# Rounding half of each query pair's phases on VectorE instead of ScalarE, in a fused attention, context and quantised-layer kernel

## The reference, cut to what matters

```python
def _fourier_kernel(x, proj_mat):
    p = jnp.einsum('blhd,dm->blhm', x, proj_mat) / math.sqrt(D_HEAD)
    return jnp.concatenate([jnp.cos(p), jnp.sin(p)], axis=-1) / math.sqrt(D_KMAP)
q = (x @ Wq.T + bq).reshape(Bv, Lv, N_HEAD, D_HEAD)
k = (x @ Wk.T + bk).reshape(Bv, Lv, N_HEAD, D_HEAD)
v = (x @ Wv.T + bv).reshape(Bv, Lv, N_HEAD, D_HEAD)
kv = jnp.einsum('blhm,blhd->bhmd', _fourier_kernel(k, proj_mat), v)
out = jnp.einsum('blhm,bhmd->blhd', _fourier_kernel(q, proj_mat), kv)
return out.reshape(Bv, Lv, D_MODEL) @ Wo.T + bo
```

## Time and profile before

| | |
|---|---|
| three runs | 1849.26 us median (1847.9 to 1851.37) |
| profiled execution | 1849.84 us, of which the span is 1848.1 us |
| mean granted clock of TensorE | 0.956 of full speed |
| PE / DVE / ACT / POOL busy | 1657.3 / 1311.1 / 1149.4 / 711.3 us |

### The profile page before, as it was taken

The page is one execution under the profiler, slowest core; times in us unless marked ns, Lnnn a source line. Parts: engine busy times, 40 slices in busy tenths (PEclk is TensorE's granted clock), DMA queues, the critical chain, the costliest instruction groups (busy, mean ns, idle before and its releaser), DMA issues. The chain is left out here.

```text
span 1848.1 us, 31958 instructions
## 1 busy us (share of the span) xinstructions
PE 1657.3 (90%) x12210; PEld 1175.4 (64%) x12210; DVE 1311.1 (71%) x1821; ACT 1149.4 (62%) x1510; POOL 711.3 (38%) x641
## 2 busy tenths in 40 slices
PE   4998998998999899899899989965698898899995
PEld 3755765675676577567467657733466776677784
DVE  4575766757667666765766767687588878888885
ACT  2595776777577577667857757755145554555564
POOL 3031212404313130340431313053286767777776
PEclk9999999999999999999999999987799999999998
DMA  4100202202011020220201102013211212222201
GB/s 152 47 24 1 70 2 69 69 1 70 25 46 44 27 70 1 69 69 1 70 24 47 42 29 70 1 46 111 80 49 56 79 63 75 74 68 74 69 35 57
DMA packets 49102, 95.87 MB, mean 52 GB/s; under 512 B 3472, under 2 KB 3792, under 8 KB 48976
## 3 DMA queue, kind: packets, MB, share of 16 engines
q1 hardware_dynamic: 38864, 76.29, 13.1%
q10 hardware_dynamic: 10112, 17.69, 2.6%
HBM read 60.38 MB, written 33.59 MB: 51 GB/s over the span
## 5 line engine op out<-in xcount | busy, mean ns | idle before, releaser
L698 DVE SCALAR_TENSOR_TENSOR feat<-feat,phases 128x1024 f32<-128x1024 f32 x256 | 301.0, 1217 | 197.2 <-ACT feat L595 197.2
L595 ACT ACTIVATE feat<-phases 128x1024 f32<-128x1024 f32 x256 | 248.3, 1023 | 217.6 <-PE phases L457 123.7
L602 ACT ACTIVATE feat<-feat 128x1024 f32<-128x1024 f32 x256 | 271.5, 1061 | 84.9 <-DVE feat L698 76.0
L385 POOL TENSOR_TENSOR ln<-moments,eps 128x4 f32<-128x4 f32 x16 | 3.2, 202 | 741.4 <-DVE moments L747 741.4
L608 ACT ACTIVATE feat<-feat 128x1024 f32<-128x1024 f32 x256 | 256.9, 1047 | 17.0 <-DVE feat L705 16.9
L705 DVE TENSOR_SCALAR feat<-feat 128x1024 int32<-128x1024 int32 x256 | 213.9, 840 | 47.9 <-ACT feat L602 47.7
L446 PE MATMUL bank<-wo_hi,att_hi 128*128 128x512 f32 x256 | 110.9, 433 | 51.3 <-DVE att_lo L731 43.0
L544 PE MATMUL kv_sum<-feat,kv_cols 128*32 128x512 f32 x1024 | 126.4, 612 | 8.6 <-ACT feat L608 8.6
L372 POOL TENSOR_TENSOR res<-res,bo_all 128x512 f32<-128x512 f32 x64 | 85.2, 1359 | 118.9 <-DMA res<-x 118.4
L446 PE MATMUL bank<-xt_hi,win_hi 128*128 128x512 f32 x256 | 109.2, 427 | 19.4 <-POOL xt_lo L363 19.4
L518 PE MATMUL kv_sum<-feat,v 128*32 128x256 f32 x2048 | 123.8, 382 | 0.0
(11 more groups left out here) (178 smaller groups left out, 4156.6 us busy)
## 6 DMA issues: line engine op xcount, KB each, us to landing
normed<-res SPq DMA_DIRECT2D x32, 513.0 KB, 4.7
xt_raw<-xT SPq DMA_DIRECT2D x16, 1024.0 KB, 6.2
res<-x SPq DMA_DIRECT2D x32, 512.0 KB, 4.2
xs<-normed SPq DMA_DIRECT2D x24, 513.0 KB, 4.1
out<-xs ACTq DMA_DIRECT2D x24, 512.0 KB, 2.8
feat<-normed SPq DMA_DIRECT2D x8, 513.0 KB, 3.8
out<-feat ACTq DMA_DIRECT2D x8, 512.0 KB, 2.8
fold<-ctx SPq DMA_DIRECT2D x8, 256.0 KB, 3.8
```

Of the source, the lines that this page charges most:

```text
L595: act.activation(feat[2 * (w % 2) + p][:, 0, :], phases[:, 2 * p:2 * p + 2, :].rearrange("p h n -> p (h n)"), ACT.Identity, bias=ROUND).th ...
L602: act.activation(f[:, 1, :], f[:, 0, :], ACT.Sin, scale=-TWO_PI).then_inc(sin_done, 1)
L698: dve.scalar_tensor_tensor(f[:, 0, :], f[:, 0, :], ROUND, phases[:, 2 * p:2 * p + 2, :].rearrange("p h n -> p (h n)"), ALU.subtract, ALU.s ...
```

## The change

In query pairs (`w >= KPAIRS`), ACT rounds only unit 0. DVE rounds unit 1 itself, with one `tensor_scalar` that reads `phases` in PSUM and writes `feat` in SBUF, at the head of its phase step, ahead of the fraction of unit 0. A new semaphore `rounded_here` orders DVE's own two instructions. Key pairs stay as they are, except for the arithmetic of the count that is waited for.

```diff
@@ ACT, kind "phase"
-                        for p in range(2):
+                        for p in range(2 if w < KPAIRS else 1):
                             act.activation(feat[2 * (w % 2) + p][:, 0, :], phases[:, 2 * p:2 * p + 2, :].rearrange("p h n -> p (h n)"),
                                            ACT.Identity, bias=ROUND).then_inc(rounded, 1)
@@ DVE, kind "phase"
                         w = s[1]
+                        if w >= KPAIRS:
+                            f = feat[2 * (w % 2) + 1]
+                            dve.wait_ge(phase_ready, PAIRS_A * own + w + 1)
+                            if w < KPAIRS + 2:
+                                dve.wait_ge(feat_used, KPAIRS * own + w - 1)
+                            dve.tensor_scalar(f[:, 0, :], phases[:, 2:4, :].rearrange("p h n -> p (h n)"), ROUND, None,
+                                              ALU.add).then_inc(rounded_here, 1)
                         for p in range(2):
                             f = feat[2 * (w % 2) + p]
-                            dve.wait_ge(rounded, 2 * (PAIRS_A * own + w) + p + 1)
+                            if p == 1 and w >= KPAIRS:
+                                dve.wait_ge(rounded_here, KPAIRS * own + w - KPAIRS + 1)
+                            else:
+                                dve.wait_ge(rounded, 3 * KPAIRS * own + (2 * w + p if w < KPAIRS else w + KPAIRS) + 1)
```

More of the change, by code:

```diff
@@ L221, in attention @@
         product_done, bank_free, hi_ready = sem("product_done"), sem("bank_free"), sem("hi_ready")
-        phase_ready, rounded, frac_ready = sem("phase_ready"), sem("rounded"), sem("frac_ready")
+        phase_ready, rounded, rounded_here, frac_ready = sem("phase_ready"), sem("rounded"), sem("rounded_here"), sem("frac_ready")
         sin_done, fold_ready = sem("sin_done"), sem("fold_ready")
```

## The result

The changed kernel takes 1882.05 us (median of 4 runs, 1880.01 to 1882.99), the kernel before 1850.32 us on the same chip. The ratio is 1.0168, with a 95% interval of 1.0148 to 1.0188: 32 us slower. The profiled executions differ by 32.9 us of span, 1881.0 against 1848.1.

The account below looks back on a forecast made before the run. PE bounds the stretch from `wo` (0,0); in pairs 8 to 12 it waits for DVE. Six loop batches 28.4 + first batch 4.2 + tail 5.2 = 37.8 us on 1849.26 gave 1887 us, 8-in-10 range 1868 to 1904.

Parts of the forecast that it names:

- The bound and the chain: Pairs 8 to 12: PE waits for the ACT-DVE chain; ACT's second rounding lies beside the first fraction, so removal gains nothing.
- The length of the addition: DVE in query pairs: 1.13 us from the added instruction's start to the fraction's; lower end 0.6, upper end 1.22.
- The cost at each pair: Query pairs: each fraction starts later by 1.13 us minus DVE's idle time ahead of it; 4.73 us a loop batch.
- the idle time: DVE's bracketed wait ahead of the fraction: 0.51 us at pair 9, none at 10, 0.22 at 11 and 12.
- The sign of the sine's wait: Sign of being right: in query pairs the sine L602 waits 0.5 to 1.1 us longer for the fraction L698.
- The first batch: First batch: 0.07 + 0.30 + 3 x 0.91 + 1.09 = 4.2 us, pair 10 taken like pairs 11 and 12.
- The tail: Last batch: pairs 8 to 11 cost 0.07 + 0.62 + 1.13 + 1.13, pairs 13 to 15 0.58, 0.51, 1.13; 5.2 us.
- pair 12, whose delay was called hidden: Tail, pair 12: delay costs nothing, since its two magnitudes take 7.20 us beside a 4.83 us POOL instruction.
- Which delays reach the end: Loop batch: pairs 8 to 12 all count, 3.64 us; 13 and 14 get through by PSUM banks, 1.09; 15 nothing.
- The clock: Rival: longer PE waits cause one more clock fall a batch, 1.8 to 2.5 us; some 1902 us, chance 0.15.
- The sum: Whole kernel: loop batches 28.4, first batch 4.2 and tail 5.2 make 37.8 us slower, forecast 1887 us.

Follow-up runs that it names:

- pairs 8 and 15: VectorE rounds unit 1 in pairs 8 and 15 alone, ScalarE in the others; ratio 1.0008 to the kernel before.
- the kernel with those two alone: VectorE rounds unit 1 in pairs 13 and 14 alone, ScalarE in the others; ratio 1.0034 to the kernel before.
- work on DVE that was worth moving: Kernel before with DVE's last normalisation of a batch moved behind pair 10: 1844.89 us; with phase ahead of output on ACT and DVE too: 1840.82 us.
- the stand-in: Kernel before plus a DVE instruction nobody reads, 1024 values from two constant SBUF rows, ahead of the query pairs' fractions; 1897.33 us, ratio 1.0265.

## Why the prediction was right

**The bound and the chain.** Right. The second rounding was free, shown twice: taken off alone it gave nothing (0.9993), and work put in its place in the changed kernel cost nothing.

**The length of the addition.** Right: 64 instructions of 1205 to 1225 ns, the fraction 1.13 us behind. The Trainium skill ("VectorE: DVE Perf Modes", "Why PSUM operands drop a tier") lets 32-bit work with a PSUM operand run in the slowest tier only. The trace agrees: the magnitude, a `tensor_scalar` of the same size within SBUF, takes 0.69 us alone.

**The cost at each pair,** 1.13 less the idle time. The rule is right, and the sizes of the exposed pairs 9 to 14 were 0.07 to 0.1 us too large:

```
             pair 8   9     10    11    12    13    14    15 (loop)
predicted    0.07    0.62  1.13  0.91  0.91  0.58  0.51  0
measured     0.09    0.53  1.06  0.81  0.81  0.49  0.43  0
```

The term mis-sized is the idle time. The bracket counts it from the recorded end of the instruction ahead, but the next one can start 0.08 us ahead of that end when it waits for nothing (619.55 against 619.63). The addition so gained 0.07 to 0.1 us at every exposed pair. For a loop batch that makes 4.2 us instead of 4.73 (pair 8's 0.09 to pair 14's 0.43), 3 us over six.

**The sign of the sine's wait.** "Larger by 0.5 to 1.1 us in query pairs" was too small. It is 99 us over 64 pairs, 1.5 each, because the gap that the rounding leaves is waiting too. The sum did not use it.

**The first batch** was mis-sized: 4.2 us predicted, 2.7 measured (0.14 + 0.21 + 0.61 + 0 + 0.82 + 0.49 + 0.43). I costed pairs 10 and 11 by the pattern of the earlier trace rows, which says nothing of POOL. In this batch POOL works beside DVE's magnitudes, and it met them at another moment in each of the two profiled executions. Those of pair 9 lasted 2.94 us before and 2.73 after. Those of pair 10, before and then after:

```profile
130.04 3.40 DVE L705 TENSOR_SCALAR feat<-feat 128x1024 int32<-128x1024 int32 x2
```

```profile
130.98 0.89 DVE L715 TENSOR_SCALAR feat<-feat 128x1024 int32<-128x1024 int32 x1
132.11 1.47 DVE L715 TENSOR_SCALAR feat<-feat 128x1024 int32<-128x1024 int32 x1 [0.24 <-ACT feat L602]
```

They ended 5.75 us behind the start of the fraction before and 4.93 after. This 0.8 us is what took pair 11's delay. It is not a property of the addition: with nothing added at all (the rounding taken off alone) pairs 10 and 11 of the first batch add -0.46 and -0.84.

**The tail:** 5.2 us predicted. Measured are 3.7 for pairs 8 to `wo` (0,0) (predicted 2.95), 0.92 for pairs 13 and 14 (predicted 1.09), and 1.14 for pair 15 at its fraction (predicted 1.13). The sum is near for a partly wrong reason. Pair 11 added 2.66 instead of 1.13, for POOL's additions met the second magnitude of pair 10 and a weight's instruction (L666) behind it. Both before, then both after:

```profile
1213.39 1.23 DVE L705 TENSOR_SCALAR feat<-feat 128x1024 int32<-128x1024 int32 x2
...
1215.19 2.28 DVE L666 TENSOR_TENSOR xt_raw<-xt_raw,winv 128x2048 f32<-128x2048 f32 x1
```

```profile
1241.89 2.32 DVE L715 TENSOR_SCALAR feat<-feat 128x1024 int32<-128x1024 int32 x2
...
1244.79 2.70 DVE L666 TENSOR_TENSOR xt_raw<-xt_raw,winv 128x2048 f32<-128x2048 f32 x1
```

That is 1.5 us, and the prediction had nothing for it but its range. Half of it is given back: pair 12, whose delay was called hidden, and `wo` (0,0) together add -0.7 us. Not all of it is due to the addition: three kernels that have none in pairs 10 to 12 (the rounding taken off alone, pairs 8 and 15, pairs 13 and 14) add 0.6 to 1.1 us at pair 11 of the tail and give 0.8 back at pair 12.

**Which delays reach the end.** Right for all seven pairs, pairs 13 and 14 included, which the kernel with those two alone confirms by itself.

**The clock.** The rival falls: what the steps add leaves no room for one more fall of 1.8 to 2.5 us a batch. Between `wo` (0,0) and phases 13 the eight batches add -0.63, 0.85, -1.42, 0.78, -0.20, 1.05, -1.31 and 0.28 us, in sum -0.6, although PE waits longer ahead (5.2 to 5.5 us in all loop batches, 3.6 to 4.3 before; 8.8 in the tail, 12.2 before). Windows of two loop batches and the tail after, to set beside the earlier trace rows:

```profile
627.80:636.00 8.20, 8.15 (x28) 6.22 (x28) 1.39 (x2) 0.00 (x0) 0.00 (x0) 0.68 0.01 2
787.00:794.20 7.20, 7.17 (x28) 5.50 (x28) 1.39 (x2) 0.00 (x0) 0.00 (x0) 0.79 0.01 2
...
1268.90:1277.30 8.40, 8.40 (x24) 6.38 (x24) 1.39 (x2) 0.00 (x0) 1.94 (x1) 0.65 0.01 2
```

The fall of the clock moves to and fro by 1.4 us, and its mean stays.

**The sum:** 28.4 + 4.2 + 5.2 = 37.8 predicted. The parts measured in the profiled execution are 25.3 (six loop batches of 4.2), 2.7 and 5.7, together 33.7. Less the 0.6 of the clock's column that is 33.1, and the execution is 32.9 us late at `wo` (1,0) of the tail. So the 6 us by which the predicted sum was high are the idle time's 3, the first batch's 1.5, less 0.5 by which the tail was low, the clock's 0.6 and 1.4 between this execution and the medians, which differ by 31.7. That the two spans differ by 32.9 too is partly luck. In the kernel with work put back on ScalarE, pair 15's fraction in the tail is 33.9 us late, and its span is only 28.9 us longer (1877.0), so the rest of the program moves by some us of its own from one execution to the next.

## What to carry to other kernels

Moving work from one engine to another pays only if the first engine is waited for at that place. Look at what ends the wait of the instruction behind it: here the sine waited for DVE and not for the rounding, so the rounding was free where it stood. What an added instruction costs is read pair by pair, as its length from start to start less the idle time ahead of its place, and the same rule, used the other way round, found work on DVE that was worth moving, though it promised twice what came. Where a third engine lengthens instructions, here POOL those of DVE, a shift of half a us moves them in or out of its way, and the rule then misses: by 0.8 us at one pair and by 1.5 at another in the changed kernel. An engine that is busy without a break is no cover where it takes buffers at the moment they are freed.

## What the runs showed of the hardware

A DVE instruction's time beside POOL depends on where it reads. The change's addition (PSUM to SBUF, 128x1024) and the stand-in of the same size (two inputs from SBUF), in the groups by line of their kernels:

```profile
L700 DVE TENSOR_SCALAR feat<-phases x64: 1205/1214/1225, 111.6 to 1300.8; 128x1024 f32<-128x1024 f32 x64
```

```profile
L700 DVE SCALAR_TENSOR_TENSOR fold<-bo_all,bv_all x64: 1207/1217/5202, 112.1 to 1316.0; 128x1024 f32<-128x1024 f32 x64
```

(shortest, median and longest, ns). The medians are alike, the longest are 1225 and 5202 ns. In each kernel 23 of the 64 stand beside one of POOL's `tensor_tensor` instructions of 128x512 or more. All 23 of the change's additions kept their length, and 21 of the 23 stand-ins lasted 1.5 us or more. Beside POOL's small instructions of 128x4 the stand-in kept its 1.22 us too. The magnitude, which reads SBUF as well, is stretched in the same way (7.20 us for two in the earlier trace rows, 0.69 each alone). The Trainium skill ("GPSIMD Engine Reference", "1. Specifications") lists the SBUF interfaces as shared with VectorE when it has two SBUF inputs or uses both ports for one, and these runs agree. An instruction that stands in for another in an experiment must therefore read from the same memory.
